# A fused transformer block on one core: the quantised projections' weights kept as scaled float16 halves

## What is computed

```
xq  = fp8(bf16(clip(layernorm(x) / in_scale)))        # four variants: q, qx, k, v, each with its own in_scale
q   = layernorm_per_head((xq_q  * q_scale)  @ wq.T  * wq_s)     # 16 heads of 128
qx  = layernorm_per_head((xq_qx * qx_scale) @ wqx.T * wqx_s)    # 16 heads
k   = layernorm_per_head((xq_k  * k_scale)  @ wk.T  * wk_s)     # 8 groups
v   =                    (xq_v  * v_scale)  @ wv.T  * wv_s      # 8 groups
kx, vx = split(cond @ w_kv_x.T);  kx = layernorm_per_head(kx)
out = fp8(concat(attend(q, k, v), attend(qx, kx, vx)) / smooth) @ wproj.T * scales
```

## Time and profile before

| | |
|---|---|
| median of three runs | 1677.27 us (1674.27 to 1680.37) |
| span of the profiled execution | 1673.7 us |
| TensorE matmul busy | 1623.2 us, 97% |
| TensorE weight load busy | 1335.0 us, 80% |
| ScalarE busy | 1102.9 us, 66% |
| VectorE busy | 1083.2 us, 65% |
| GpSimd busy | 485.3 us, 29% |
| attention, first query matmul to last | 492 to 1503 us of the span |

### The profile page before, as it was taken

One profiled execution on the slowest core, in us unless ns is written; L12 is line 12 of the kernel. 1 busy time (PEld: TensorE's weight loads), 2 busy tenths in 40 slices (PEclk: granted clock), 3 DMA queues, 4 the chain that ended last, 5 costly groups with the idle time before them and its releaser, 6 DMA issues.

```text
span 1673.7 us, 27163 instructions
## 1 busy us (share of the span) xinstructions
PE 1623.2 (97%) x9136; PEld 1335.0 (80%) x9136; DVE 1083.2 (65%) x2115; ACT 1102.9 (66%) x2983; POOL 485.3 (29%) x515
## 2 busy tenths in 40 slices
PE   7989989999999999999999999999999999999998
PEld 6878756666778888888788888888888788887887
DVE  6258855445985767777777776566666666788322
ACT  4364245553559888888888887878778787885100
POOL 1001122224424424334243343342433433330000
PEclk9999989999999999999999999999999999999999
DMA  7031649995772143283342362121152121110011
GB/s 271 26 107 41 258 151 325 311 316 187 243 270 80 54 183 104 92 333 109 113 182 89 133 264 83 57 88 57 57 218 79 44 108 56 38 45 1 25 38 38
DMA packets 75156, 220.72 MB, mean 132 GB/s; under 512 B 6368, under 2 KB 14560, under 8 KB 68640
## 3 DMA queue, kind: packets, MB, share of 16 engines
q1 hardware_dynamic: 69360, 200.61, 33.1%
q0 software_dynamic: 5680, 18.62, 3.6%
HBM read 158.65 MB, written 60.56 MB: 131 GB/s over the span
## 4 chain that ended last, share of the span: by engine, by line
PE 78%; DVE 4%; ACT 4%; issue 1%; DMA 1%; POOL 1%; ACTq 0%; POOLq 0%; SPq 0%; DVEq 0%
PE bank L2478 10%; PE bank L2479 10%; PE bank L97 7%; PE bank L2541 7%; PE bank L99 7%; PE bank L98 7%; PE bank L2559 6%; PE bank L2572 6%; PE bank L2530 5%; PE bank L1388 4%; PE bank L1408 4%; PE bank L2551 3%; PE bank L1368 1%; DVE x_res L1747 1%; ACT t_sc L2699 1%
## 5 line engine op out<-in xcount | busy, mean ns | idle before, releaser
L2810 DVE TENSOR_TENSOR t_hn<-bank,t_rs 128x256 f32<-128x256 f32 (+1 forms) x256 | 130.7, 552 | 140.1 <-POOL t_rs L2443 72.7
L2478 PE MATMUL bank<-t_slot,t_x_q 128*128 128x512 f32 x512 | 205.8, 402 | 0.0
L2440 POOL TENSOR_SCALAR t_ve<-t_ss 128x4 f32<-128x4 f32 (+1 forms) x128 | 25.9, 202 | 616.4 <-DVE t_ss L2806 608.9
L2479 PE MATMUL bank<-t_slot,t_x_q 128*128 128x512 f32 x512 | 200.2, 391 | 0.0
L2699 ACT ACTIVATE t_sc<-bank,t_mx 128x128 f32<-128x128 f32 x512 | 183.9, 455 | 3.5 <-DVE t_mx L2830 3.5
L2443 POOL TENSOR_TENSOR t_rs<-t_ve,t_mhalf 128x4 f32<-128x4 f32 (+1 forms) x128 | 171.0, 1336 | 10.6
L2699 ACT ACTIVATION_READ_ACCUMULATOR t_sc<-bank,t_mx 128x1 f32 x512 | 151.6, 296 | 0.0
L2737 ACT ACTIVATE t_y<-bank,smooth 128x128 bf16<-128x128 f32 x512 | 139.3, 401 | 1.9 <-PE bank L2559 1.9
L2541 PEld LDWEIGHTS bank<-t_hT 128*128 128x128 f32 x1024 | 120.1, 191 | 16.8 <-ACT t_hT L2726 16.2
L2541 PE MATMUL bank<-t_hT 128*128 128x128 f32 x1024 | 131.0, 281 | 2.3 <-ACT t_hT L2726 2.3
L2479 PE MATMUL bank<-t_slot,t_x_kv 128*128 128x256 f32 x512 | 125.6, 283 | 0.0
(11 more groups left out here) (344 smaller groups left out, 4159.1 us busy)
## 6 DMA issues: line engine op xcount, KB each, us to landing
t_slot<-w_ready SPq DMA_DIRECT2D x16, 2048.0 KB, 9.8
t_xh<-xq_scratch SPq DMA_DIRECT2D x64, 512.0 KB, 3.6
t_cr<-in_ctxT_dram SPq DMA_DIRECT2D x64, 256.0 KB, 2.7
y_rows<-s_y SPq DMA_DIRECT2D x39, 256.0 KB, 3.2
e_w<-in_w_units_dram SPq DMA_DIRECT2D x8, 1024.0 KB, 12.4
w_rows<-in_w_qkv_dram SPq DMA_DIRECT2D x8, 1024.0 KB, 6.2
w_ready<-w_hi SPq DMA_DIRECT2D x8, 1024.0 KB, 6.3
w_ready<-w_lo SPq DMA_DIRECT2D x8, 1024.0 KB, 6.1
```

Source lines behind the costliest of these rows:

```text
L2478: nc.tensor.matmul(out, x_in[:, k, :], w[0][:, k, a:b], start=k == 0, stop=False)
L2479: last = nc.tensor.matmul(out, x_in[:, k, :], w[1][:, k, a:b], start=False, stop=k == KT - 1)
L2810: nc.vector.tensor_tensor(hn[:, lo:hi, :], b3[bk][:, 0:hi - lo, :], rs[:, lo:hi].unsqueeze(2).broadcast_to([P, hi - lo, P]), ALU.mult).the ...
```

## The change

The weights of the four quantised projections are stored as float16 halves (`w_half`), and only the context segment stays fp32r (`w_plain`). So that the halves keep their precision, each projection's weights are multiplied by a power of two found at run time: a new table of the input scales (1 MB, `scales`) is loaded at the start, its maximum is taken, and the exponent gives `factor` and its inverse `sigma`. Everything that reads the projections from PSUM multiplies by `sigma`: the squares (`squares_a`, part 0, and `squares_b`) and the values (part 0) get a scale that is a per-partition pointer, where the scale was a constant, and the head weights of q, qx and k are multiplied by it once. `rows_kv` and `rows_q` are gone, with their semaphores: TensorE takes `xh` as the stationary operand and float16 weights as the moving one. The load of `xh` for sequence `m`, which waited for the two copies of `m-2`, now waits for the queries of `m-2` on TensorE. Each weight block is stored by four DMAs and no longer two, with 1.25 MB in place of 2 MB; the low half has one buffer instead of two, so VectorE waits until the low half of the block before is stored (`lo_free`), and ScalarE's `hi_part` now also waits for it in the early blocks. Scaled constants (`wfac`, `q_wb`) move from `constants()` to `half_constants()`, after `low(2)`.

```diff
-                     self.hi[:].bitcast(FP32).rearrange("p (s n) -> p s n", s=4)).then_inc(self.hi_st, 16)
+                     self.hi[:].rearrange("p (s n) -> p s n", s=3)).then_inc(self.hi_st, 16)
+        sp.dma_start(self.dram_plain[quarter, :, 0, k, :], self.hi_rest[:].bitcast(FP32)).then_inc(self.hi_st, 16)
...
-                     self.lo[n % len(self.lo)][:].bitcast(FP32).rearrange("p (s n) -> p s n", s=4)).then_inc(self.lo_st[n % 2], 16)
+                     self.lo[:].rearrange("p (s n) -> p s n", s=3)).then_inc(self.lo_st[n % 2], 16)
+        sp.dma_start(self.dram_plain[quarter, :, 1, k, :], self.lo_rest[n % 2][:].bitcast(FP32)
+                     ).then_inc(self.lo_st[n % 2], 16)
...
-            act.wait_ge(self.hi_st, 16 * n)
-            if len(self.lo) == 1:
-                act.wait_ge(self.lo_in, n)
+            act.wait_ge(self.hi_st, self.STORED * n)
+            act.wait_ge(self.lo_in, n)
         for _, a, b, f in self.SEGS:
             self.nc.scalar.activation(self.hi[:, a:b], rows[:, a:b], ACT.Copy,
                                       scale=self.env.wfac[:, f * KT + k:f * KT + k + 1])
-        self.nc.scalar.activation(self.hi[:, self.PLAIN:], rows[:, self.PLAIN:], ACT.Copy).then_inc(self.hi_in, 1)
+        self.nc.scalar.activation(self.hi_rest[:], rows[:, self.PLAIN:], ACT.Copy).then_inc(self.hi_in, 1)
+
+    def lo_free(self, dve, n):
+
+        if n:
+            dve.wait_ge(self.lo_st[(n - 1) % 2], self.STORED * ((n - 1) // 2 + 1))
 
     def lo_part(self, dve, n):
-        rows, lo, k = self.rows[n % 2], self.lo[n % len(self.lo)], self.where(n)[1]
+        rows, lo, k = self.rows[n % 2], self.lo, self.where(n)[1]
         dve.wait_ge(self.hi_in, n + 1)
-        if len(self.lo) == 1 and n:
-            dve.wait_ge(self.lo_st[(n - 1) % 2], 16 * ((n - 1) // 2 + 1))
+        self.lo_free(dve, n)
...
-                                                self.hi[:, a:b].bitcast(FP32), ALU.mult, ALU.subtract)
-        self.nc.vector.tensor_tensor(lo[:, self.PLAIN:], rows[:, self.PLAIN:],
-                                     self.hi[:, self.PLAIN:].bitcast(FP32), ALU.subtract).then_inc(self.lo_in, 1)
+                                                self.hi[:, a:b], ALU.mult, ALU.subtract)
+        self.nc.vector.tensor_tensor(self.lo_rest[n % 2][:], rows[:, self.PLAIN:], self.hi_rest[:].bitcast(FP32),
+                                     ALU.subtract).then_inc(self.lo_in, 1)
...
+        if segs[0] is self.SEGS[0]:
+            self.lo_free(dve, n)
...
+        def half_constants():
+            ins, steps = env.cols("in_scale"), self.halves
+            dve.wait_ge(self.scales_in, 16)
+            v.tensor_reduce(self.most[:], self.scales[:], op=ALU.max, axis=AX.X, apply_absolute_value=True
+                            ).then_inc(steps, 1)
+            dve.wait_ge(steps, 1)
+            v.tensor_tensor(self.most[:], self.most[:], env.cols("w_scale"), ALU.mult).then_inc(steps, 1)
+            dve.wait_ge(steps, 2)
+            v.tensor_scalar(self.power[:], self.most[:].bitcast(U32), EXPONENT, None, ALU.bitwise_and).then_inc(steps, 1)
+            dve.wait_ge(steps, 3)
+            v.tensor_scalar(self.inverse[:], self.power[:], EXPONENT, None, ALU.bitwise_xor).then_inc(steps, 1)
+            v.tensor_scalar(env.sigma[:], self.power[:].bitcast(FP32), 1.0 / (ROOM * DOWN), None, ALU.mult
+                            ).then_inc(steps, 1)
+            dve.wait_ge(steps, 5)
+            v.tensor_scalar(self.factor[:], self.inverse[:].bitcast(FP32), ROOM / 2, None, ALU.mult).then_inc(steps, 1)
+            for i, (out, n) in enumerate(((env.q_wb[:, 0:1], 0), (env.q_wb[:, 2:3], 4))):
+                v.tensor_scalar(out, env.col("head_wb", n), SCALE, env.sigma[:, i:i + 1], ALU.mult, ALU.mult
+                                ).then_inc(steps, 1)
+            v.tensor_tensor(env.k_w[:], env.col("head_wb", 2), env.sigma[:, 2:3], ALU.mult).then_inc(steps, 1)
+            dve.wait_ge(steps, 6)
             for i in range(4):
                 v.tensor_scalar(env.wfac[:, i * KT:(i + 1) * KT], ins[:, i * KT:(i + 1) * KT], env.col("w_scale", i),
-                                1.0 / DOWN, ALU.mult, ALU.mult).then_inc(steps, 1)
-            for n in (0, 4):
-                v.tensor_scalar(env.q_wb[:, n // 2:n // 2 + 2],
-                                env.par[:, COLS["head_wb"][0] + n:COLS["head_wb"][0] + n + 2], SCALE, None,
-                                ALU.mult).then_inc(steps, 1)
-            v.scalar_tensor_tensor(env.coef[:, 0:1], env.col("proj_scale", 0), 1.0 / DOWN, env.col("proj_scale", 1),
-                                   ALU.mult, ALU.mult).then_inc(steps, 1)
-            dve.wait_ge(steps, 18)
-            v.tensor_tensor(env.coef[:, 1:2], env.coef[:, 0:1], env.gate_tanh[:, 1:2], ALU.mult).then_inc(steps, 1)
+                                self.factor[:, i:i + 1], ALU.mult, ALU.mult).then_inc(steps, 1)
...
         low(2)
+        half_constants()
         added(1)
...
     slots = [sb(f"slot{i}", kb, [P, 2, KT, D], F32R) for i, kb in enumerate(SLOTS)]
+    halves16 = [sb(f"half{i}", kb, [P, 2, KT, D], F16) for i, kb in enumerate(SLOTS)]
...
-    x_q = sb("x_q", 100, [P, 2, KT, P], F32R)
...
-    x_kv = sb("x_kv", 160, [P, 2, KT, P], F32R)
...
             if m >= 2:
-                sp.wait_ge(xkv_in, m - 1)
-                sp.wait_ge(xq_in, m - 1)
+                sp.wait_ge(b_ps, (m - 1) * 2)
...
         def weights(quarter, seg, loaded):
-            sp.dma_start(slots[homes[quarter][seg]][:].bitcast(FP32), ready.dram[quarter, (2, 3, 0, 1)[seg]]
-                         ).then_inc(loaded, 16)
+            home = homes[quarter][seg]
+            if seg == KVX:
+                sp.dma_start(slots[home][:].bitcast(FP32), ready.dram_plain[quarter]).then_inc(loaded, 16)
+            else:
+                sp.dma_start(halves16[home][:], ready.dram[quarter, {KV: 2, WQ_: 0, WQX: 1}[seg]]).then_inc(loaded, 16)
...
-            slot = slots[homes[quarter_of(m, quarter)][seg]]
+            slot = (slots if seg == KVX else halves16)[homes[quarter_of(m, quarter)][seg]]
             return slot[:, 0], slot[:, 1]
 
-        def project(out, w, a, b, x_in):
+        def project(out, w, a, b, rows, kind):
             for k in range(KT):
-                nc.tensor.matmul(out, x_in[:, k, :], w[0][:, k, a:b], start=k == 0, stop=False)
-                last = nc.tensor.matmul(out, x_in[:, k, :], w[1][:, k, a:b], start=False, stop=k == KT - 1)
+                nc.tensor.matmul(out, rows[:, k, kind, :], w[0][:, k, a:b], start=k == 0, stop=False)
+                last = nc.tensor.matmul(out, rows[:, k, kind, :], w[1][:, k, a:b], start=False, stop=k == KT - 1)
             return last
 
-        def keys_values(m, quarter):
+        def keys_values(m, par, quarter):
             w = halves(m, quarter, KV)
             if opens(m):
                 pe.wait_ge(kv_w, 16 * (m // B + 1))
-            pe.wait_ge(xkv_in, m + 1)
+            pe.wait_ge(xh_in[par], (m - par) * 8 + 16)
             if later(m, 1):
                 pe.wait_ge(n_in, m * 4 - 3)
             else:
                 pe.wait_ge(sh.x_in, C * J - 1)
-            project(bank[2][:, 0:256], w, 256, 512, x_kv[:, 0])
-            project(bank[2][:, 256:512], w, 0, 256, x_kv[:, 1]).then_inc(a_ps, 1)
+            project(bank[2][:, 0:256], w, 256, 512, xh[par], 2)
+            project(bank[2][:, 256:512], w, 0, 256, xh[par], 3).then_inc(a_ps, 1)
 
         def context_keys_values(m, quarter):
...
-            pe.wait_ge(xq_in, m + 1)
             if later(m, 1):
                 pe.wait_ge(e_in, m * 3 - 1)
-            project(bank[0][:], halves(m, quarter, WQ_), 0, D, x_q[:, 0]).then_inc(b_ps, 1)
+            project(bank[0][:], halves(m, quarter, WQ_), 0, D, xh[par], 0).then_inc(b_ps, 1)
             if opens(m):
                 pe.wait_ge(qx_w, 16 * (m // B + 1))
             if later(m, 1):
                 pe.wait_ge(e_in, m * 3)
-            project(bank[1][:], halves(m, quarter, WQX), 0, D, x_q[:, 1]).then_inc(b_ps, 1)
+            project(bank[1][:], halves(m, quarter, WQX), 0, D, xh[par], 1).then_inc(b_ps, 1)
...
-        def rows_kv(m, par):
-            act.wait_ge(xh_in[par], (m - par) * 8 + 16)
-            if later(m, 1):
-                act.wait_ge(a_ps, m * 2 - 1)
-            env.carry(act)
-            nc.scalar.activation(x_kv[:], xh[par][:, :, 2:4, :].rearrange("p k v s -> p v k s"), ACT.Copy
-                                 ).then_inc(xkv_in, 1)
-
-        def rows_q(m, par):
-            if later(m, 1):
-                act.wait_ge(b_ps, m * 2)
-            env.carry(act)
-            nc.scalar.activation(x_q[:], xh[par][:, :, 0:2, :].rearrange("p k v s -> p v k s"), ACT.Copy
-                                 ).then_inc(xq_in, 1)
-
         def wproj(quarter, part):
             i, a = divmod(part, 2)
...
-                nc.scalar.activation(sqk[:, part * QG:part * QG + QG, :], b3[2 + part][:, 0:2, :], ACT.Square
```

(19 more changed lines are left out.)

88 lines of the change are left out of this document (52 added, 36 removed).

## The result

| kernel | median of the runs | profiled span | ratio to before, 95% interval |
|---|---|---|---|
| before | 1678.8 us (1674.3 to 1681.2) | 1673.7 us | 1 |
| changed | 1652.0 us (1648.7 to 1652.2) | 1650.4 us | 0.9840 [0.9820, 0.9861] |

The account below looks back on a forecast made before the run. TensorE was taken as the bound. Gains of 21.5 (55 steps), 4.6 (seven chain-bound steps), 0.2, 0.3 and 0.2 make 26.8 us: profiled 1673.7 to 1646.9, plus 3.6 gives a median of 1650.5 us; range 1643 to 1661.

Parts of the forecast that it names:

- Queries and keys: TensorE's projection matmuls: float16 spacing 215 and 109 ns, 0.39 us less per TensorE-bound step, 21.5 us over 55 steps.
- Chain-bound steps: Seven steps waiting for normalised heads: ScalarE's chain 0.65 us shorter each (bounds 0.39 and 0.95), 4.6 us in all.
- The waits: TensorE's seven waits for normalised heads: still there, each about 0.25 us shorter.
- the seven: Steps 1 to 3, step 7 and three later steps with `wproj` copies, where TensorE waits 7.9 us for normalised heads.
- Step 8: Step after step 7: GpSimd waits 3.05 us for context rows beside a 2 MB load; 0.3 us gained with 1 MB.
- Loads of the rows: `x_rows` waits for queries of `m-2`; later loads queue behind on SyncE. Cost nothing, 5.5 us cover in worst case seen.
- Rival C: SyncE's wait before `x_rows`: the load of `xh` becomes the bound, kernel slower, 1693 us at 16.2 us landing; chance 0.03.
- Start and weight preparation: Before the first queries: scales load and `half_constants` cost 0 (3 without cover); weight preparation taken as 0.
- step 0: First step: the first keys' gain vanishes because context matmuls wait 3.8 us for VectorE; 0.2 us gained.
- the 2.6 allowed: Routed stage of weight preparation: less DMA could remove TensorE's idle 0.5 + 2.1 us; gain 0 to 2.6, taken as 0.
- The stretch behind the last queries: After the last first-query matmul: the last queries add 0.2 us of gain.
- ScalarE: ScalarE busy time over 64 steps: two copies gone, four pointers added at 0.1 us each; down some 110 us.

Follow-up runs that it names:

- the second group: The changed kernel unaltered, measured again beside three variants on one chip with shared runs of before (1674.36 us): 1645.87 us, ratio 0.9827.
- the second trace of the changed kernel: Profile of the unaltered changed kernel from its repeat measurement: profiled span 1648.1 us; median of those runs 1645.87 us, ratio to before 0.9827.
- the experiment: Changed kernel with the rows' load issued after the step's scores, 3.45 us before TensorE needs the rows instead of 15.5: 1718.45 us, ratio to before 1.0241.
- the streams: Separate kernel computing no layers: TensorE matmul streams in float16 and fp32r, ScalarE copies and squares with constant or pointer scale; no total time or ratio given.
- the second kernel with late rows: Changed kernel with the rows loaded after the scores, except in five steps of each quarter where segment loads queue: 1666.34 us, ratio to before 0.9931.

## Why the prediction held, and where it did not

The forecast was a gain of 26.8 us. It was right in sign, in main cause and, to some three microseconds, in size (23.3 by the profiles). That the medians give 26.8 to the digit is luck: against the 1677.3 us that the prediction started from the gain is 25.2, and in the second group it is 28.5. Point by point, by the profiles:

- **Queries and keys.** Forecast 0.39 us per TensorE-bound step and 21.5 for 55 of them. Measured 0.356 for 51 steps, 0.40, -0.05 and 0.31 in steps 4 to 6, and as much of step 8: 19.2. The spacings were right (215.8 and 109.2 ns for 215 and 109). The sum was 0.03 per step too high, for two reasons. The spacings were rounded: 16 x (228.8 - 215.8) and 16 x (119.5 - 109.2) ns are 0.37 us, and the second trace of the changed kernel shows just that (15.867 to 15.491). In the first trace the context's fp32r matmuls, which now follow float16 ones, took 0.02 more: 2.542 us for eleven of their spacings against 2.520 before, and 2.518 in the second trace. Why they did so in one trace only is open. Step 5 is the other part: I costed no chain for it, and one 0.2 us below TensorE's time was there.
- **Chain-bound steps.** The size of 0.65 was right: 0.68, 0.68, 0.62, 0.68, 0.68 us in steps 2, 3, 7, 35, 51, and the experiments take it apart into 0.93 for `x_kv` and 0.29 for the pointers. The set was wrong. In step 1 the copy isn't on the chain: ScalarE itself waits 2.24 us for VectorE's maxima before the exponentials, so the step had no 0.95 to gain (before without the copies it is as long as before), and lost 0.17 to the pointers. Step 19 got its shorter chain, and gave it back by a half-clock stretch of 1.55 us (19.21 against 17.66 with the same wait and full clock, in the kernel with the late rows). 4.6 forecast, 2.3 measured.
- **The waits.** Forecast 0.25 us shorter in each of the seven. Steps 2, 3 and 7: 0.89 to 0.58, 1.29 to 1.01, 1.02 to 0.63, right. Steps 19, 35 and 51 grew, 1.60 to 1.75 in the first; but there TensorE also waited for the probabilities before (those transposes took 1.33 us by their starts, 0.87 after), which the earlier trace rows doesn't show and I had missed: 0.46 less and 0.15 more is 0.3. The row of before in step 19:

```profile
803.86 0.66 PE L2551 MATMUL bank<-ident,t_sc 128*128 128x128 f32 x4 [0.24 <-DVE t_sc L2839]
```

  Step 1 grew by 0.53, from 0.46 to 0.99: 0.36 that TensorE gained and could not use, and the pointers.
- **Step 8.** 0.65 less, 0.36 as every step and 0.29 for the smaller segment loads beside the context rows; forecast 0.3. That the loads are the cause of the 0.29 is argued from one fact, that GpSimd has no wait for `t_cr` there now; the row that answers to the earlier trace rows:

```profile
610.48 1.50 POOL L2467 TENSOR_SCALAR t_c_hi<-t_cr 128x512 fp32r<-128x512 f32 x1
```

- **Loads of the rows.** No wait for `t_xh`, as forecast, and the longest landing is 6.2 us. But the prediction called the work behind SyncE's wait harmless because it moves by 2 us; the experiment shows that a shift of 12 us is far from harmless, and that the segments, more than the rows, were the danger. Rival C had the right place and watched the wrong load.
- **Start and weight preparation.** `half_constants` takes 53.15 to 57.29, 4.1 us, and TensorE has no wait between 40 and 80 us, neither here nor before the change: cost nothing, as forecast:

```profile
53.15 2.28 DVE L534 TENSOR_REDUCE a_most<-a_scales 128x4 f32<-128x2048 f32 x1
...
57.29 0.68 DVE L509 TENSOR_TENSOR a_a_T<-bank,a_a_T 128x512 f32<-128x512 f32 x1
```

 The first query matmul came 2.75 us earlier. I can't give that to the change: the three traces of the changed kernel have it at 489.2, 488.8 and 488.8, before and before without copies at 492.0 and 491.3, but kernels with the same code up to there as the changed one at 482.6 (`wp` copies moved) and 491.5 (rows loaded later in part). What differs between them is, among other things, how long TensorE stood at half clock. In the trace of before one such stretch of 6.8 us begins at 485.7, and the twelve context matmuls ahead of the first queries fall into it:

```profile
486.74 0.77 PE L97 MATMUL bank<-t_slot,t_c_hi 128*128 128x512 f32 x1 [3.82 <-DVE x_res L1736]
```

 They take 491.997 - 486.74 = 5.25 us there; in the first trace of the changed kernel they begin at 486.42 and take 2.83 with the full clock, and that is 2.4 of the 2.75 us. In its second trace the half clock is back and they take 4.42. The row also shows a misreading of the prediction: the wait of 3.8 us for VectorE, by which it put step 0 at 0.2, ends ahead of the first query matmul and isn't in step 0. In the windows of the earlier trace rows the DMA share fell from 0.95 to 0.82 and from 0.78 to 0.68, and TensorE's busy time rose by 0.47 and 0.23 us:

```profile
300.00:345.00 45.00, 45.00 (x199) 31.16 (x198) 22.30 (x39) 23.46 (x55) 13.17 (x11) 1.00 0.82 272
345.00:390.00 45.00, 43.16 (x179) 28.66 (x178) 16.05 (x26) 25.36 (x52) 6.89 (x7) 1.00 0.68 225
```

 That is at most 0.7 us of the 2.6 allowed. Step 0 gave 1.4 us back. In the three traces of the changed kernel it took 16.6, 15.5 and 17.1, with waits for VectorE's `z_xn` of 0.90, none and 1.38 us, so it hangs on where VectorE is. In sum 1.3 for these two parts, 0.2 forecast. The stretch behind the last queries gained 0.1 for 0.2.
- **ScalarE** is 91 us less busy; forecast some 110, though the product given for it, 64 x (1.06 + 1.19 - 0.4), is 118. The four pointers cost 0.09 us each as forecast, but the copies were taken by their durations, and records of neighbours overlap (1.08 us long, the next one 0.95 us later, in the earlier trace rows). By their starts the copies are 0.95 each and the balance is 64 x (1.90 - 0.37) = 98. The last 7 us are open.
- **From the profile to the runs.** I added the 3.6 us by which the median stood above the profiled execution. It was 1.6 for the changed kernel. Two errors cancel here: the gain by profiles is 3.5 us below the forecast, the median 1.5 us above it.

## What to carry to other kernels

When the busiest engine leaves no hole, the spacing of its instructions by form, read off the starts, predicts a change of their type, here to a tenth of the gain; work on any other engine was worth nothing there, and its full length in most of the steps that waited for a chain through that engine. Count these steps one by one from their own waits, and ask which near-bound steps a faster engine uncovers. A wait put ahead of one load delays all that its queue issues behind it, and most of the price can come from those, here two thirds, and not from the load that waits.

## What the runs showed of the hardware

- An fp32r matmul follows the one before it after 226.7 ns at 512 moving columns and 120 at 256, a float16 one after 215.8 and 109.2. The surcharge of 11 ns is the same at both sizes and doesn't depend on the stationary columns (128 or 32). After a change of type the first six fp32r matmuls with 512 columns come at 224 to 236 ns; with four and four in turn an fp32r matmul costs 236. A change of size does the same: in the kernel before, the context's matmuls, fp32r behind fp32r ones of 256 columns, come at 233, 236, 229, 232 and 231 ns before they settle at 227.
- A scale pointer costs a ScalarE instruction 92 ns, at 256 and 512 elements, for copy and square. The Trainium skill, "ScalarE: Activation LUTs", section "What ACT_TABLE_LOAD costs", gives about 93 ns for each pointer operand; the streams agree.
- After a wait of 1.74 to 1.79 us in step 19 TensorE was granted 1.2 GHz for 3.4 us in four of six profiled executions: in all three of the changed kernel, and in the second kernel with late rows. It isn't the wait alone: the kernel with all rows late has the same wait of 1.75 us in that step and its full clock, and so has the kernel with the copies kept, idle for 0.72 and 1.79 us there. Steps 35 and 51 of the changed kernel, with waits of 1.46 to 1.50 us, never had it, nor had step 19 with 1.48 us in the kernel without pointers. What decides between these was not found.
- The stretch up to the first query matmul varies by up to 9 us between profiled executions whose code there is the same (482.6 to 491.5 us), while an ordinary step repeats to 0.05 us. Small gains are read from the steps, not from the span.
